# Zero fills begin twelve chunks later; last two softmax exponentials behind more gate chunks; last gathers on the SP queue

## The reference, cut to what matters

```python
OFFSETS = sorted(set(range(33)) | {48, 64, 96, 128, 192, 256, 384, 512, 768, 1024, 1536})
q, k, v = heads(split(layernorm(x) @ qkv_w.T + qkv_b))
for i, o in enumerate(OFFSETS):
    lg = (q * shift(k, o)).sum(-1) / 8 * (1 + q @ scale_embed[i]) + pos_bias[i]
p = softmax(stack(lg), -1)                      # 44 probabilities per token and head
out = sum(p[..., i] * shift(v, o)) * if_gain
gate = sigmoid(layernorm(x) @ gate_w.T + gate_b)
x = x + layernorm((out * gate) @ out_w.T + out_b)
x = x + layernorm(layernorm(x) @ W.T + bias)    # W unfolded from two small factors
```

## Time and profile before

| what | us |
| --- | --- |
| three runs | 728.51, 731.53, 776.9; median 731.53 |
| the profiled execution | 731.03 |
| span of its slowest core (core 0) | 729.1 |
| spans of the other cores | 719.3 to 728.6 |
| PE, DVE, ACT, POOL busy on core 0 | 600.9, 431.9, 342.0, 272.9 |

### The profile page before, as it was taken

One profiled execution on the slowest core, in us unless ns is written; L12 is line 12 of the kernel. 1 busy time (PEld: TensorE's weight loads), 2 busy tenths in 40 slices (PEclk: granted clock), 3 DMA queues, 4 the chain that ended last, 5 costly groups with the idle time before them and its releaser, 6 DMA issues.

```text
span 729.1 us, 15108 instructions; the slowest of 8 cores (719.3 to 729.1 us)
## 1 busy us (share of the span) xinstructions
PE 600.9 (82%) x5408; PEld 312.8 (43%) x5408; DVE 431.9 (59%) x772; ACT 342.0 (47%) x480; POOL 272.9 (37%) x282
## 2 busy tenths in 40 slices
PE   1899969999989999999993496738788888888864
PEld 0444434444434555555541364535344444444431
DVE  4455555322232377788825367545458888888872
ACT  3566654333323655556531362624554545454532
POOL 3088888300000324332242445603424544445120
PEclk9999989999999999999996799857899999999996
DMA  8948997556575687898774988599314545553311
GB/s 211 237 151 224 281 272 249 181 178 204 127 147 161 186 204 209 202 245 207 184 173 75 164 205 208 151 247 248 89 51 127 172 146 170 150 167 106 116 58 58
DMA packets 73977, 126.49 MB, mean 173 GB/s; under 512 B 31116, under 2 KB 34316, under 8 KB 73392
## 3 DMA queue, kind: packets, MB, share of 16 engines
q1 hardware_dynamic: 51136, 71.06, 36.6%
q0 software_dynamic: 8608, 24.47, 17.1%
q10 hardware_dynamic: 14160, 30.00, 11.5%
HBM read 85.39 MB, written 50.59 MB: 187 GB/s over the span
## 4 chain that ended last, share of the span: by engine, by line
PE 46%; DVE 20%; DMA 9%; issue 8%; POOL 8%; ACT 5%; SPq 2%; DVEq 1%; ACTq 0%; POOLq 0%
PE ps L318 17%; PE ps L347 14%; PE ps L481 4%; DVE stt L262 4%; DVE stt L263 4%; PE ps L834 3%; DVE rq L852 3%; POOL rq L236 2%; DVE stt L884 2%; PE ps L499 2%; POOL rq L238 2%; SPq L62 2%; PE ps L613 2%; DMA simg<-rs 2%; DMA rk<-plimg 2%
## 5 line engine op out<-in xcount | busy, mean ns | idle before, releaser
L318 PE MATMUL ps<-ry,rw 128*128 128x512 f16 x832 | 194.6, 387 | 23.4 <-ACT rx L664 12.0
L318 PEld LDWEIGHTS ps<-ry,rw 128*128 128x128 f16 x832 | 79.2, 100 | 117.5 <-issue 33.2
L376 DVE CAST rs<-ps 128x896 f16<-128x896 f32 x32 | 34.7, 1090 | 81.1 <-PE ps L395 74.7
L613 PE MATMUL ps<-idb,rk 128*112 128x128 f16 x512 | 42.4, 236 | 41.8 <-DVE rk L376 25.1
L376 POOL COPY rk<-rk 128x896 f16<-128x896 f16 x28 | 50.3, 1804 | 70.2 <-PE ps L613 67.1
L347 PE MATMUL ps<-rw,ry 128*128 128x512 f16 x320 | 75.5, 380 | 0.0
L667 POOL TENSOR_SCALAR ry<-rx,cst 128x512 f16<-128x512 f32 x32 | 35.1, 1101 | 81.7 <-ACT rx L664 81.7
L834 PE MATMUL ps<-rw 128*128 128x512 f16 x256 | 63.0, 391 | 0.0
L834 PE MATMUL ps<-rq,rw 128*128 128x512 f16 x256 | 62.2, 387 | 0.0
L376 DVE COPY rk<-rk 128x896 f16<-128x896 f16 x36 | 35.5, 1027 | 43.0 <-DMA rk<-pcimg 22.3
L613 PEld LDWEIGHTS ps<-idb,rk 128*112 128x112 f16 x512 | 38.5, 144 | 51.8 <-issue 47.1
(11 more groups left out here) (109 smaller groups left out, 1024.6 us busy)
## 6 DMA issues: line engine op xcount, KB each, us to landing
rk<-vimg SPq DMA_DIRECT2D x64, 224.0 KB, 5.4
rx<-xs SPq DMA_DIRECT2D x18, 512.0 KB, 9.7
rq<-xs SPq DMA_DIRECT2D x16, 512.0 KB, 5.0
out<-rq SPq DMA_DIRECT2D x16, 512.0 KB, 2.7
plimg<-zt ACTq DMA_DIRECT2D x7, 1024.0 KB, 19.6
simg<-rs SPq DMA_DIRECT2D x32, 224.0 KB, 2.9
pcimg<-zt ACTq DMA_DIRECT2D x7, 1024.0 KB, 4.7
vimg<-rv ACTq DMA_DIRECT2D x28, 256.0 KB, 3.6
```

The costliest lines, as they stand in the source:

```text
L318: mm = op("tensor", lambda e, ic=ic, wof=wof: e.matmul(ps[:, b * 512:(b + 1) * 512], w[:, wof:wof + 128], yt[:, yo + ic * 512:yo + (ic + 1 ...
L376: return op(eng, lambda e: e.tensor_copy(dst, src), *waits)
L613: tp = op("tensor", lambda e, h=h: e.transpose(bass.AP(ph, b * 1024 + h * 128, [[8192, WK], [1, 128]]), sv(rk, PH + (hh * 8 + h) * WK, [1, ...
```

## The change

Three edits. The zero fills are issued at k = 6 to 21 (after chunks 27 to 87) in place of k = 3 to 18 (chunks 15 to 75). The exponential of softmax_a becomes a call of its own, `softmax_e`, which for units 14 and 15 stands behind four and two more gate chunks. `gather(15)` goes to the SP queue, in front of the raw_loads of s = 16, on a third set of semaphores.

```diff
@@ -439,7 +439,7 @@
                 w_step(k)
             if 1 <= k < 5:
                 wqt[k - 1] = w_part(rw1, "wq", k - 1, mm, y1t_tok[3 + k])
-            if k >= 3:
+            if k >= 6:
                 zero_fill(mm)
         if chunk is k_chunk:
             lastk = mm
@@ -508,22 +508,22 @@
         return mm
 
     def gather(v):
-        s = v % 2
+        s, eng, sm = v % 2, *(("gpsimd", v % 2) if v < NU - 1 else ("sync", 2))
         for k in range(2):
-            gl = dma("gpsimd", f"gl{s}",
+            gl = dma(eng, f"gl{sm}",
                      sv(rw1, s * 784, [1, 16 * LRUN], p0=k * 64, np_=64),
                      bass.AP(t["simg"], (2 * v + k) * SKEW, [[32 * SKEW, 64], [1, 16 * LRUN]]),
                      *(sdone[q] for q in range(NQ)), s1done.get(v - 2), lastq)
         for k in range(2):
-            gc = dma("gpsimd", f"gc{s}",
+            gc = dma(eng, f"gc{sm}",
                      sv(rw1, 1568 + s * 752, [1, 16 * CRUN], p0=k * 64, np_=64),
                      bass.AP(t["cimg"], (2 * v + k) * 64 * ROW, [[SKEW, 64], [1, 16 * CRUN]]),
                      cdone[v], s1done.get(v - 2))
-        gp = dma("gpsimd", f"gp{s}", PM[s], t["pbm"].ap()[v], s1done.get(v - 2), lastq)
+        gp = dma(eng, f"gp{sm}", PM[s], t["pbm"].ap()[v], s1done.get(v - 2), lastq)
         gath[v] = (gl, gc, gp)
 
     mxd, Zd, rzd = (smx[:, 16 * i:16 * i + 16] for i in range(3))
-    expt = {}
+    expt, dif = {}, {}
 
     def softmax_a(v):
         s = v % 2
@@ -546,7 +546,11 @@
         m = op("vector", lambda e: e.tensor_reduce(mxd, T3, AX.X, ALU.max), s1done[v])
         mb = sv(smx, 0, [1, 16], [0, NS])
         d = op("vector", lambda e: e.tensor_tensor(T3, T3, mb, ALU.subtract), m)
-        expt[v] = op("scalar", lambda e: e.activation(T, T, AF.Exp), d)
+        dif[v] = d
+
+    def softmax_e(v):
+        T = TB[v % 2]
+        expt[v] = op("scalar", lambda e: e.activation(T, T, AF.Exp), dif[v])
 
     def softmax_b(v):
         P_, T = PP[v % 2], TB[v % 2]
@@ -731,6 +735,7 @@
         if s < 16:
             if s >= 2:
                 softmax_a(s - 2)
+                softmax_e(s - 2)
             lastqk = coarse_qs(s)
             if s >= 2:
                 v_next(1)
@@ -739,6 +744,7 @@
         elif s < 19:
             if s == 16:
                 v_next(len(vwork))
+                gather(15)
                 prfree[0] = prfree[1] = (lastqk,)
                 vbfree[0] = vbfree[1] = vbfree[2] = lastqk
                 phfree[0] = phfree[1] = lastqk
@@ -748,12 +754,23 @@
                     raw_load(u, scat[u])
                 for u in range(3):
                     v_load(u)
-            g_next(2)
             if s < 18:
                 softmax_a(s - 2)
-            softmax_b(s - 3)
-            scatter(s - 3)
-            g_next(2 if s < 18 else 1)
+            if s == 16:
+                softmax_b(13)
+                scatter(13)
+                g_next(4)
+                softmax_e(14)
+            elif s == 17:
+                g_next(4)
+                softmax_b(14)
+                scatter(14)
+            else:
+                g_next(2)
+                softmax_e(15)
+                softmax_b(15)
+                scatter(15)
+                g_next(1)
             for i in range((s - 16) * 3, min((s - 15) * 3, 8)):
                 wol = dma("gpsimd", "wol", wo_[:, i * 1024:(i + 1) * 1024],
                           bass.AP(t["wo"], i * 1024, [[8192, 128], [1, 1024]]), lastqk)
@@ -778,7 +795,7 @@
                 wbl = dma("gpsimd", "wbl", wbig[:, (w - 12) * 4096:(w - 11) * 4096],
                           bass.AP(t["wbimg"], (w - 12) * 4096, [[8192, 128], [1, 4096]]),
                           bank_v[0], wst["free"][0], wst["free"][1])
-        if s + 1 - 2 in range(NU):
+        if 0 < s < 16:
             gather(s - 1)
         if s < 16 and s - 3 in range(NU):
             softmax_b(s - 3)
```

## The result

The changed kernel takes 731.83 us (median of 20 runs, 729.37 to 744.23) against 729.84 for the kernel before (20 runs): ratio 1.0037, 95% interval 1.002 to 1.0054. Forecast were 719.5 us and a range of 713.5 to 725.5. Single executions disturbed by a slower clock on one die are left out of the ratios.

A forecast was written before the change was run, and what follows sets the result against it. PE's chain was taken as the bound, with stops in the projection and at the softmax end (12.04 and 9.32 us). 731.03 - 14.0 (softmax) + 0 (fills, front) + 2.5 (fills, back) = 719.5 us, range 713.5 to 725.5.

The forecast's parts named there:

- The softmax part: End of the softmax: gather(15) on SP and later exponentials bring class_turn(2) from 418.07 to 404.1, -14.0 us, bounds 12 to 16.
- the landing of gather(15): Softmax end: gather data taken to land at 374.8, upper bound 380, leaving 5 us of slack.
- softmax_b(15) at 390.7: Softmax end: exp(15) ends at 387.9 behind gate chunks, so softmax_b(15) ends at 390.7, the next late step.
- then SP's eight issues: After softmax_b(15), SP issues scatter(15)'s eight DMAs, done by 397.3, before raw_load(2).
- the issue of a scatter: SP at the softmax end: 6.6 us per scatter, bounds 4.6 to 7.5.
- All that follows 418 depends on queue order alone: After class_turn(2): everything later moves as a block, so the softmax gain reaches the end, with the distance still 311 us.
- rival 3: Stages after 418 give back half of the 14 us, since something there was on time only by lateness: 726.5; chance 0.06.
- The fills, back: Projection end: three late fills beside the wv loads delay wv, the simg store and PE's restart, +2.5 us, range 0 to 6.4.
- The restart at lower clock (2.74 us for 8 matmuls, rows 2) is paid already: PE's restart behind the wv loads: its slow clock was already in the time before, so nothing was added.
- rival 2: Fills take full turns against the wv loads: +6.4 us at 214, softmax gain unchanged, 723.4; chance 0.15.
- The fills, front: Projection front: wq stop shrinks from 6.7 to 4 to 6 us, lost again at chunk n = 51; worth 0, bound 1.5.
- Rival 4: Middle stage: v stores stuck behind fills on the ACT queue stop ACT and PE; slower, +4.4 us, 735.5; chance 0.04.

The follow-up runs named there:

- e3: The changed kernel with a buffer of its own for unit 15's probabilities, so softmax_b(15) doesn't wait for scatter(13); ratio to the kernel before 0.9961.
- e14: The changed kernel itself run again, beside its two parts alone on the same chip; ratio to the kernel before 0.9983.
- e10: The changed kernel with zero fills back at k = 3 to 18 and an own buffer for unit 15's probabilities; ratio to the kernel before 0.9900.
- e2: The changed kernel with zero fills back at k = 3 to 18, so the softmax part alone; ratio to the kernel before 0.9900.
- e16: Repeat of e2, the softmax part alone with zero fills at k = 3 to 18, on another chip; ratio to the kernel before 0.9900.
- e4: The changed kernel with the eight wo loads issued one per step at s = 20 to 27, not s = 16 to 18; ratio to the kernel before 1.0035.
- e6: The changed kernel with early fills (k = 3 to 18), own buffer for unit 15, v_loads behind scatter(13), wo loads from s = 20; ratio to before 0.9939.
- e1: The kernel before with only the zero fills moved, to k = 6 to 21; ratio to the kernel before 1.0077.
- e8: The kernel before with zero fills from k = 6, two each at k = 12 to 14, the last at k = 18; ratio to the kernel before 1.0026.
- e15: Repeat of e1, the kernel before with only the zero fills moved to k = 6 to 21, on another chip; ratio to the kernel before 1.0102.
- e5: The changed kernel with v_load(0) to (2) called behind scatter(13) on SP, not ahead of it; ratio to the kernel before 0.9955.

## Why the prediction was wrong

**The softmax part: the step failed that named what is late next.** Its times up to softmax_b(15) hold: begun at 388.06 on core 2 and 387.09 on core 5, forecast 387.9; the landing of gather(15) had slack. "softmax_b(15) at 390.7" failed, with "then SP's eight issues" behind it. Two things are wrong in it. The first is a wait left out, `scat.get(v - 2)`, which the code shows and the profile of before could not, since there scatter(13) was issued from 376.65 and asked for only by the last instruction of softmax_b(15), at 399.15 (core 0, SP):

```profile
376.65 2.39 SPq L62 DMA_DIRECT2D plimg<-rw  x4
```

Moving softmax_b(15) up by some 10 us brought it up against that DMA. The second is the term that was mis-sized, the issue of a scatter: 6.6 us, bound 7.5; measured 5.3 to 12.0 for scatter(13) and 5.8 to 13.0 for scatter(14) in the changed kernel. I took the duration from a stretch in which two scatters met five wo loads, while in the new order two scatters meet eight, with v_loads. The trace of before had a warning: scatter(13) took 5.6 to 10.9 us there over the eight cores, 6.4 on the one I read. The second error is the one that costs: taking only the wait away gained nothing (e3 beside e14, e10 beside e2 and e16), while with scatters of 4.5 to 5.4 us class_turn(2) came 35.9 us after the last value chunk (e4), and 35.7 in e6, as forecast.

The sum for this part was -14.0 with bounds -12 to -16; measured -9.5 and -8.4 on the mean of cores. In distances from the last value chunk to class_turn(2), on the mean of cores: forecast 35.0; e2 37.6 and e16 38.7, so slow scatters cost about 3 us of it. Another 2 us lie in the starting point: 48.5 in the profile of before (49.0 on core 0), but 46.0 to 47.0 in e1, e8 and e15, which have the old order at the end of the softmax. On cores that the wait spares the forecast distance is there: 34.4 us on core 5 of the changed kernel, 33.6 to 35.3 on four cores of e2.

**"All that follows 418 depends on queue order alone" failed in part.** In the changed kernel's profile, class_turn(2) to the first projection takes 90.7 us on the mean of cores (88.3 before), up to 94.5; in e14, the same kernel, 89.6, and in e2 88.5. This was rival 3, at 0 to 2 us rather than 7; its cause is open.

**The fills, back: right place, wrong size.** wv and the simg store did move, on the mean of cores by 4 us of the second wv load's landing and 2.5 of the longest store. The price is 3.3 us at the restart and 1.3 behind it, 5 to 6 by the timed runs, against +2.5. The restart's own term was short by about 1 us. The larger error that can be located is the sentence "The restart at lower clock (2.74 us for 8 matmuls, rows 2) is paid already": that held for core 0, which I read, and for no other core; cores 3 and 4 had no stop before, and five stopped and restarted at the usual 1.9 us. With late fills seven of the eight restart slowly. The total of 5 to 6 lies toward the upper bound of 6.4, but not by rival 2's way, which put all 6.4 at the restart. The Trainium skill (DMA: Bandwidth & Descriptors, section Queues, rings and completion order) has each DMA engine take turns between the queues, a whole packet at a time; no run here shows the size of a turn, so the 3.3 us speak neither for nor against it.

**The fills, front: nothing won, as forecast.** Chunk n = 51 starts between 137.7 and 141.1 on all cores (138.3 to 140.3 before). That the stop for wq would shrink isn't shown: it is 6.4 in place of 6.8 us on the mean of cores, and within a job it is no shorter with late fills (5.0 and 5.1 in e15 and e14, 4.2 in e16, whose fills are early).

**The metric.** I worked on one core. The time is the slowest of eight: the change's mean of cores in e14's job is 2.9 us below before, the slowest only 1.0. The wait for scatter(13) strikes some cores by 5 to 13 us and spares others, so it costs the slowest core more than the mean. Rival 4 (v stores stuck behind fills) is not seen: the v stores up to 260 land in 2.0 to 8.3 us (2.4 and up to 8.5 on core 0 before). Summed up by the runs on the mean of cores: -8.9 (e2 and e16) + 5.6 (e1 and e15) = -3.3, beside the measured -2.9 (e14). The slowest core's -1.0 in e14 and the +2.7 of the 20 runs' ratio hold the spread of the cores besides, which this sum doesn't give.

## What to carry to other kernels

When a step is pulled forward, list every token it waits for in the code, also those that were satisfied long before, and put each one's new time beside it: here a buffer's last reader, a DMA two units back, was the first to be met. Then test whether that wait is a cause or a sign: a buffer of its own removed it and gained nothing, because what stood behind the slow DMAs on the same queue was just as late. Traffic moved out of one crowded stretch costs in the next if that is crowded too; look in the windows view for a stretch with a DMA share near 0 and try it there. Size a stall, and the starting point too, on all cores and if possible in more than one execution, since a stall that strikes a few of them costs more when the slowest core is the metric.

## What the runs showed of the hardware

The issue time of a DMA on SP isn't fixed: the same eight scatter DMAs took 4.5 to 4.6 us for scatter(15) of the changed kernel, with little else in flight, and 4.5 to 5.4 for all scatters of e4, and up to 13.0 (changed kernel, core 3) and 15.1 (e5, core 3) beside fp32-to-fp16 loads and v_loads. What stands behind them on SP is late by as much. Taking the wo loads away brought the time back to 4.5 to 5.4 us; by what the queue is held isn't shown.

One program's cores differ in one and the same execution: softmax_b(15) waited 12.56 us for scatter(13) on core 2 of the changed kernel and not at all on core 5, and in e14, the same kernel, the stops behind the gate chunks ran from 3.4 to 8.6 us.

The clock can fall over a stop of a few us, and doesn't always. Core 3 of e1 stood 4.16 us ahead of the value chunks and was granted 0.50 from 219 to 223, so that eight matmuls took 3.57 us in place of 1.90. Core 5 of the changed kernel stood 3.57 us there, kept 1.00, and the eight took 1.90:

```profile
217.00:221.00 4.00, 4.00 (x48) 1.85 (x48) 3.00 (x3) 0.59 (x1) 0.00 (x0) 1.00 0.80 257
```
